# An output stage without transpositions: normalising attention in its own layout, with inverted sums spread by one bf16 product

## What is computed

```python
h = _layernorm(x) * (1 + ca) + sa
# attention with rope and causal mask, per head of 16 channels
scores = einsum('bhid,bhjd->bhij', q, k) / sqrt(16), masked
out = einsum('bhij,bhjd->bhid', softmax(scores), v) @ Wo + bo
x = x + ga * (h + out)                    # per batch: ga is a row of 256
h = _layernorm(x) * (1 + cb) + sb
x = x + gb * experts(h)                   # 8 experts, 512 tokens each
```

## Time and profile before

| | us |
|---|---|
| median of three runs | 3014.26 (3013.57 to 3014.30) |
| the profiled execution | 3013.66 |
| its span | 3011.9 |

### The profile page before, as it was taken

How to read it: one execution, slowest core, us unless ns; L and a number is a source line. 1 busy time by engine, 2 the same in 40 slices (tenths; PEclk the granted TensorE clock), 3 DMA queues, 4 the chain that set the end, 5 groups by cost and what they waited for, 6 DMA issues and landing times. The chain is left out here.

```text
span 3011.9 us, 48208 instructions
## 1 busy us (share of the span) xinstructions
PE 2753.8 (91%) x17467; PEld 1341.3 (45%) x17467; DVE 2140.9 (71%) x3145; ACT 1825.3 (61%) x3739; POOL 974.6 (32%) x1298
## 2 busy tenths in 40 slices
PE   1788889499999999999999999999999879998997
PEld 0454445234444444444444444444444346775664
DVE  4999999587777777777777777777777436652221
ACT  1676677157777777777777777777777744441121
POOL 1666666312212212212212212212211247771331
PEclk7899999689999999999999999999999989999999
DMA  3367676824454354454454455354345068962342
GB/s 97 119 221 231 220 233 210 214 50 93 87 108 93 88 106 94 87 106 94 88 105 95 89 104 99 86 103 98 88 102 102 25 227 291 312 224 58 99 109 44
DMA packets 186485, 384.09 MB, mean 128 GB/s; under 512 B 33397, under 2 KB 102421, under 8 KB 173736
## 3 DMA queue, kind: packets, MB, share of 16 engines
q1 hardware_dynamic: 180106, 372.48, 48.2%
q0 software_dynamic: 6144, 8.52, 1.6%
HBM read 238.55 MB, written 144.53 MB: 127 GB/s over the span
## 5 line engine op out<-in xcount | busy, mean ns | idle before, releaser
L929 DVE TENSOR_REDUCE mx<-ps 128x2 f32<-128x1024 f32 (+3 forms) x1216 | 1371.5, 1167 | 396.9 <-PE ps L1017 301.7
L975 ACT ACTIVATE prob<-ps 128x512 f32<-128x512 f32 (+1 forms) x2560 | 1251.8, 560 | 538.8 <-PE ps L1035 530.1
L1010 PE MATMUL ps<-k_rows,q_rows 96*128 96x512 bf16 (+3 forms) x3072 | 911.2, 332 | 41.0 <-DMA k_rows<-k_parts 34.4
L1035 PE MATMUL ps<-q_rows,k_rows 99*128 99x512 bf16 (+3 forms) x3072 | 907.2, 328 | 14.7 <-ACT prob L975 6.1
L868 POOL TENSOR_SCALAR_AFFINE_SELECT prob<-prob 128x512 f32<-128x512 f32 x512 | 320.0, 637 | 1451.3 <-ACT prob L975 1451.3
L1054 PE MATMUL ps<-prob,v_rows 128*32 128x512 f32 (+3 forms) x6144 | 628.3, 496 | 0.0
L1035 PEld LDWEIGHTS ps<-q_rows,k_rows 99*128 99x128 bf16 x3072 | 273.1, 98 | 599.0 <-ACT prob L975 360.3
L1010 PEld LDWEIGHTS ps<-k_rows,q_rows 96*128 96x128 bf16 x3072 | 290.2, 98 | 271.4 <-DVE mx L929 60.5
L1017 PE MATMUL ps<-mask_b,unit_b 128*128 128x128 bf16 (+2 forms) x1408 | 348.6, 248 | 0.0
L673 PE MATMUL ps<-x_t,w_all 128*128 128x512 f32 x512 | 249.8, 634 | 0.0
L1054 PEld LDWEIGHTS ps<-prob,v_rows 128*32 128x32 f32 x6144 | 134.3, 108 | 245.8 <-ACT prob L975 122.9
(11 more groups left out here) (154 smaller groups left out, 2678.1 us busy)
## 6 DMA issues: line engine op xcount, KB each, us to landing
k_rows<-k_parts SPq DMA_DIRECT2D x384, 128.0 KB, 7.3
v_ones<-v_st SPq DMA_DIRECT2D x64, 512.0 KB, 4.3
v_rows<-v_ones SPq DMA_DIRECT2D x64, 512.0 KB, 9.1
att<-o_sb SPq DMA_DIRECT2D x128, 256.0 KB, 2.4
att_b<-att SPq DMA_DIRECT2D x16, 2048.0 KB, 10.1
q_parts<-stage SPq DMA_DIRECT2D x128, 192.0 KB, 3.3
k_parts<-stage SPq DMA_DIRECT2D x128, 192.0 KB, 3.3
q_rows<-q_parts SPq DMA_DIRECT2D x64, 384.0 KB, 4.6
```

Source lines behind the costliest of these rows:

```text
L929: dve.tensor_reduce(dst, src, AX.X, ALU.max).then_inc(a_free, 1)
L975: nc.scalar.activation(prob[:, (g * NPC + i) % RING, h, 0:w], src, ACT.Exp).then_inc(exp_done, 1)
L1010: ins = pe.matmul(ps[:, at, col:col + w], q[0:ROWS, g, h, i * P:(i + 1) * P], k[0:ROWS, g, h, k0:k0 + w], start=(r == 0), stop=True, skip_ ...
L1035: ins = pe.matmul(ps[:, PS_B + bank(g, n), at:at + w], k[0:AUG, g, h, j * P:(j + 1) * P], q[0:AUG, g, h, q0:q0 + w], start=True, stop=True)
```

## The change

The output stage keeps tokens along the columns throughout, as `att_d` has them and as the output product wants them, so nothing is transposed and the copy of L1332 goes. Attention rows and sums are loaded apart. The sums of a batch come as 128 partitions of 128 columns, are inverted there in one instruction, split in three bf16 parts, stored to DRAM and loaded again as 48 rows (3 parts x 16 heads) of 1024 tokens. A product of these 48 rows with a constant matrix of ones and zeros puts each head's inverse on the 16 rows of its channels in PSUM, 512 tokens at a time, two such products for the two halves of the channels, so four a batch. VectorE multiplies the attention rows with it. Inverses are formed three batches ahead, products of spread inverses and normalising run one batch ahead of the output product, in between its tiles.

The depth of the output product's PSUM ring grows from 2 banks to 4, x is kept for 3 batches and not 4, the residual may run two batches ahead of the sums, in place of ScalarE's two tiles ahead of its copies. The residual's instructions, the norm of the chosen tiles and the experts stay as they are.

```diff
@@ SP's queue @@
+            def load_den(b):
+                reuse(sp, inverted, b - 1)
+                sums = att_d[b].rearrange("g (h n) t -> (g h) n t", n=2 * DH)[:, DH, :]
+                sp.dma_start(den[:, b % 2, :], sums.rearrange("h (a c) -> h a c", c=P)).then_inc(den_in[b % 2], DMA)
+            def save_inv(b):
+                sp.wait_ge(inv_done, b + 1)
+                sp.dma_start(rec_d[b].rearrange("s h (a c) -> (h a) s c", c=P), inv3[:, b % 2]).then_inc(inv_stored[b % 2], DMA)
+            def load_rec(b):
+                sp.wait_ge(inv_stored[b % 2], (b // 2 + 1) * DMA)
+                reuse(sp, spread, (b - RR + 1) * NQ)
+                sp.dma_start(rec[:, b % RR, :], rec_d[b].rearrange("s h t -> (s h) t")).then_inc(rec_in[b % RR], DMA)
+            def load_num(b):
+                reuse(sp, norm_done, (b - 1) * NQ)
+                for k in range(KC):
+                    mine = att_d[b, k * NG // KC:(k + 1) * NG // KC].rearrange("g (h n) t -> (g h) n t", n=2 * DH)
+                    sp.dma_start(num[:, b % 2, k, :], mine[:, 0:DH, :]) \
+                      .then_inc(num_in[b % 2], DMA)
...
+            load_den(0)
+            load_den(1)
+            load_small(0)
+            load_num(0)
+            save_inv(0)
+            load_den(2)
+            load_rec(0)
+            load_x(0)
+            save_inv(1)
+            load_num(1)
...
             for b in range(B):
+                if b + 2 < B:
+                    load_small(b + 2)
+                    load_num(b + 2)
+                if b + 3 < B:
+                    save_inv(b + 3)
+                if b + 4 < B:
+                    load_den(b + 4)
                 if b + XR - 1 < B and b >= 1:
-                    load_x(sp, b + XR - 1)
+                    load_x(b + XR - 1)
+                if b + 3 < B:
+                    load_rec(b + 3)
...
+                store(b)
@@ VectorE @@
+            def invert(b):
+                p = b % 2
+                dve.wait_ge(den_in[p], (b // 2 + 1) * DMA)
...
+                dve.reciprocal(inv[:, p, :], den[:, p, :]).then_inc(inverted, 1)
...
+                dve.tensor_copy(inv3[:, p, 0, :], inv[:, p, :]).then_inc(inv_hi, 1)
...
+                dve.tensor_tensor(inv_rest[:, p, :], inv[:, p, :], inv3[:, p, 0, :], ALU.subtract).then_inc(inv_left, 1)
...
+                dve.tensor_copy(inv3[:, p, 1, :], inv_rest[:, p, :]).then_inc(inv_mid, 1)
...
+                dve.tensor_tensor(inv3[:, p, 2, :], inv_rest[:, p, :], inv3[:, p, 1, :], ALU.subtract).then_inc(inv_done, 1)
+            def normalise(b, q):
...
+                dve.wait_ge(spread, b * NQ + q + 1)
+                dve.tensor_tensor(n_t[:, b % 2, k, at], num[:, b % 2, k, at], ps[:, PS_R + q % 2, :], ALU.mult) \
+                   .then_inc(norm_done, 1)
...
+            for b in range(B):
+                if b + 1 < B:
+                    scale_weights(b + 1)
+                for t in range(T):
+                    if t == 1 and b + 3 < B:
+                        invert(b + 3)
+                    finish(b, t)
+                    prepare((b - SB) * T + t)
+                    if t % 2 == 1 and b + 1 < B:
+                        normalise(b + 1, t // 2)
@@ ScalarE @@
-                    reuse(act, x2_done, b * T - T)
+                reuse(act, x2_done, (b - 2) * T + t + 1)
...
-                    nc.scalar.copy(n_t[:, t % 2], ps[:, PS_T + t % 2, 0:D].rearrange("p (k n) -> p k n", k=KC)) \
-                      .then_inc(nt_copied, 1)
@@ TensorE @@
+            def spread_rec(b, q):
...
+                pe.matmul(ps[:, PS_R + q % 2, :], mine, rec[:, b % RR, half * HALF:(half + 1) * HALF],
+                          start=True, stop=True).then_inc(spread, 1)
+            def product(b, t):
...
+                pe.matmul(o, ones3[:, :], ob[:, b % 4, :], start=True, stop=False)
+                for k in range(KC):
+                    ins = pe.matmul(o, n_t[:, b % 2, k, t * P:(t + 1) * P], wg[:, b % 2, k, :], start=False,
+                                    stop=(k == KC - 1))
...
+            for b in range(B):
+                for t in range(T):
+                    product(b, t)
+                    if t % 2 == 0 and b + 1 < B:
+                        spread_rec(b + 1, t // 2)
```

More of the change, by code:

```diff
@@ L1147, in phase3 @@
         pair = lambda n: (sem(n + "0"), sem(n + "1"))
[L1148 to L1158, removed]
+        num = sb("num", [P, 2, KC, L], F32)
+        den = sb("den", [P, 2, P], F32)
+        inv = sb("inv", [P, 2, P], F32)
+        inv_rest = sb("inv_rest", [P, 2, P], F32)
+        inv3 = sb("inv3", [P, 2, 3, P], BF16)
+        rec = sb("rec", [3 * HEADS, RR, L], BF16)
+        rows = sb("head_rows", [3 * HEADS, HEADS, DH], BF16)
+        unit3 = sb("unit3", [3 * HEADS, HEADS], F32)
         st = sb("st4", [P, NT, 6], F32)
@@ L1177, in phase3 @@
         block = ctx.enter_context(nc.Block())
[L1179 to L1184, removed]
-        def load(sp, b, p):
-            sp.dma_start(gate[:, p], mods_d[b, M_GA, :].partition_broadcast(P)).then_inc(small_in[p], DMA)
-            sp.dma_start(ob[:, p], out_bias_d[b]).then_inc(small_in[p], DMA)
-            sp.dma_start(att[:, p], att_d[b].rearrange("g p t -> p g t")).then_inc(att_in[p], DMA)
@@ L1200, in store @@
+            def store(b):
                 sp.wait_ge(x2_done, b * T + T)
-                sp.dma_start(dst.rearrange("(t p) d -> p t d", p=P), x2[:, p]).then_inc(stored[p], DMA)
+                dst = sum_d[b * L:(b + 1) * L] if b < SB else out[b]
+                rows2 = ffn.x2[:, b * T:(b + 1) * T, :] if b < SB else x2[:, b % 2]
+                sp.dma_start(dst.rearrange("(t p) d -> p t d", p=P), rows2).then_inc(stored[b % 2], DMA)
             def load_chosen():
@@ L1298, in _ @@
-            loop(dve, work)
+            for b in range(2):
+                invert(b)
+            dve.wait_ge(unit_in, 3 * DMA)
+            dve.tensor_copy(rows[:, :, :], unit3[:, :].rearrange("p (h o) -> p h o", o=1)
+                            .to_broadcast([3 * HEADS, HEADS, DH])).then_inc(rows_done, 1)
+            invert(2)
+            scale_weights(0)
+            for q in range(NQ):
+                normalise(0, q)
+            for b in range(B):
[8 more added lines that the diff above has]
+                        normalise(b + 1, t // 2)
@@ L1401, in _ @@
-            loop(pe, work)
+            def spread_rec(b, q):
+                k, half = q % KC, q // KC
+                n = b * NQ + q
+                if q == 0:
+                    pe.wait_ge(rec_in[b % RR], (b // RR + 1) * DMA)
+                reuse(pe, norm_done, n - 1)
+                mine = rows[:, k * (HEADS // KC):(k + 1) * (HEADS // KC), :].rearrange("p h n -> p (h n)")
+                pe.matmul(ps[:, PS_R + q % 2, :], mine, rec[:, b % RR, half * HALF:(half + 1) * HALF],
+                          start=True, stop=True).then_inc(spread, 1)
```

170 lines of the change are left out of this document (79 added, 91 removed).

## The result

The changed kernel takes 3038.37 us (median of four runs, 3035.77 to 3041.27) against 3014.28 for the kernel before on the same chip: ratio 1.0078, 95% interval 1.0066 to 1.0091. It is 24 us slower where 34 us faster was forecast. The profiled execution took 3038.47 us (span 3036.4).

A forecast was written before the change was run, and what follows sets the result against it. GpSimd was to become the output stage's bound in TensorE's place: start 2445.4 + work 218.7 + collisions 10.4 + lag 5 + last sum 0.5 + what follows 300.6 = 2980.6, said as 2980 us, range 2964 to 3000.

The forecast's parts named there:

- The step that failed: Output stage, DMA: a batch moves 3.66 MB, at 333 GB/s 11.0 us, hidden with 2 us to spare.
- The second step that failed: SP's queue: waits after the start are covered, since x is issued two batches, some 25 us, before GpSimd wants it.
- rival (b): Output stage: DMA or SP's order bounds; 2990 us at 265 GB/s, 3000 with waits on top; chance 0.13.
- its work with the collisions: GpSimd in the output stage: 218.7 us of work, plus 10.4 us for collisions with thirteen inverts.
- its waits: GpSimd in batches 2 and 3: a lag behind VectorE's bn_stats and bn_aggr comes due, 5 us, from 0 to 8.
- what follows: Everything after the output stage's last sum: 300.6 us, not touched by the change.
- TensorE: Output stage: 1.27 us a tile without transpositions, four spreading products 1.3 us a batch; sum 11.4 us a batch.
- Rival (c): TensorE, now waiting for others in each tile, is granted the lower clock; 3036 us; chance 0.05.
- Rival (d): Inverses aren't there when TensorE spreads them, each batch waits some 3 us; about 3010 us, no change; chance 0.04.
- VectorE: Output stage: reciprocal 0.95 us, normalising pieces 0.687 us each, invert with collisions 3 us a batch.
- Collision with GpSimd: Beside VectorE's invert GpSimd loses 0.43 of the other's length, 0.8 us an invert, 10.4 us in all, from 4 to 31.
- Start: Output stage: GpSimd starts at 2445.4, 2 us later than before, as x waits behind the first inverses; bounds 2444 and 2448.

The follow-up runs named there:

- e8: Changed kernel with channels ordered (n, head), so the outermost dimension of each attention load is 16 and not 8; 2983.9 us.
- e4: Changed kernel with five idle products of 48 rows and 256 columns behind each tile; 3231.6 us.
- e5: Changed kernel with five idle products of 128 rows and 256 columns behind each tile, on values of the output weights; 3049.8 us.
- e13: Changed kernel with only the bias product padded by zeros from 3 rows to 128; 3040.9 us.
- e14: e8 with two idle products of 128 rows and 256 columns behind each tile; 2985.6 us.
- e2: Changed kernel with a batch's attention rows in sixteen loads of 16 rows in place of two; 3004.4 us.

## Why the prediction was wrong

**The step that failed** is the DMA's: "3.66 MB, at 333 GB/s 11.0 us ... Hidden, with 2 us to spare". The rate was read from loads of another shape. The new attention loads have 8 heads as the outermost dimension of their source, and while they run almost alone the share is 0.51 and the rate 173 GB/s, against 1.01 and 405 for the old ones. In the stage the 3.66 MB went at 227 GB/s, which makes 16.1 us a batch and not 11.0. The Trainium skill (DMA: Bandwidth & Descriptors, "Why a DMA increments its semaphore by 16 and not by 1") says that a transfer is dealt to as many engines as the largest number up to 16 that divides the slowest dimension of both its sides, here 8. This case's trace agrees: the share is 0.51, and the single change of that dimension to 16 brought it to 1.03 and gave 54.6 us. Both loads of a batch are on the way in that stretch and the share is still a half, which speaks for the same eight engines. What the loads take from the eight engines that all transfers need can be estimated: of 3.66 MB a batch 1.05 lie on one half alone, so that half carries 1.05 + 2.61 / 2 = 2.35 MB, as if 4.7 MB were moved, more than the 4.45 of before. The saving in bytes, on which the DMA sum rested, was gone. And 333 GB/s was too high even for loads on all engines: e8 has 273 in the stage, 13.4 us a batch. In the packets of the trace a row of 4 KB took 161 ns in the mean while the old loads ran alone (2434 to 2437 us), 183 after (2436 to 2441), 269 in e8 (2435.5 to 2440).

**The second step that failed**: "Later waits of this kind are covered: SP issues x two batches, some 25 us, before GpSimd wants it". The residual now runs up to two batches ahead of the sums itself, so this lead is spent: from SP's issue of x to the moment when GpSimd is through with the batch before, the trace has 12.1 us (median of batches 3 to 15; 42.9 in the kernel before). ScalarE could start only 15.7 us after the issue, and GpSimd waited 66.5 us in 12 batches, 5.5 each. In e8 the two are 13.2 and 10.2, and the wait is nearly gone. SP's wait for the store of the inverses in each round, 83.7 us in all, stood in rival (b) and was put at nothing in the sum: the prediction had the 9.0 us landing of small stores and used it only for the start.

By the sum's own terms, as times of the last sum:

| term | forecast | after | e8 |
|---|---|---|---|
| GpSimd's start | 2445.4 | 2450.05 | 2449.39 |
| its work with the collisions | 229.1 | 217.9 | 218.4 |
| its waits | 5 | 66.5 | 14.6 |
| to the end of the last sum | 0.5 | 2.5 | 0.5 |
| last sum ends | 2680.0 | 2737.0 | 2682.9 |
| what follows | 300.6 | 301.5 | 300.6 |

- **TensorE**: 1.27 us a tile at the high level is right (the sums of the last tiles of the kernel after stand 1.27 apart). A tile with a spreading product takes 1.59, so such a product costs 0.32, the 0.22 and 0.1 of the sum. The clock was not priced: with the transpositions it stood at 1.00, without them at 0.78. That their 128 rows had kept it up is argued from e4 and e5; no run shows it.
- **Rival (c)**, chance 0.05, named the fall of the clock and drew the wrong consequence. The clock did fall, to 0.78 of full speed. Waiting, the reason that (c) gave, isn't enough: in e4 TensorE hardly waited (busy 222 of 230 us) and the level was low throughout. And a stage that waits for DMA hides it: with 37 us less to do for TensorE (e13) the time moved by +2.1. That the measured 3038 lies near (c)'s 3036 is chance. The argument against (c), the clock of 0.91 at 31 of 40 us busy, did not carry over: TensorE was busy for the same 78% here, with other products.
- **Rival (b)**, chance 0.13, named the right place, DMA and SP's wait for the store, and priced it at 2990 to 3000, from the average rate of the old transfers. Its own rate was again one of full spread. The measured 227 GB/s was below every rate that it took.
- **Rival (d)**, chance 0.04: its sum is wrong in itself. Sixteen batches at 3 us are 48 us and not the 30 that it adds.
- **VectorE**: the reciprocal took 950 ns (0.95 forecast), the normalising 674 (0.687). The five steps of an invert came to 2.63 us in the mean, in e8 to 3.02 (3 forecast).
- **Collision with GpSimd**: over-sized. The row at 2559.35, from which 0.43 was taken, has the addition itself stretched from 0.415 to 0.76 us (it starts at 2558.92), and at its median of 0.748 it was mostly VectorE that lost. From before to after the mean of the residual's operations went from 753 and 731 ns to 753 and 735, that of the scalings from 728 to 794: 1.6 us in all, where 10.4 were put in. In e8 it is 2.3.
- **Start**: 2449.4 to 2450.05 for 2445.4. The store of the first inverses, issued at 2435.12, landed after 7.3 us and not 3.1, behind the loads of `num`, and x after it.

```profile
2435.12 0.38 SPq L1198 DMA_DIRECT2D rec_sums<-inv  x1
...
2442.44 0.30 SPq L1203 DMA_DIRECT2D rec<-rec_sums  x1
...
2450.05 0.73 POOL L1413 TENSOR_TENSOR res_b<-res_b,a_b 128x256 f32<-128x256 f32 x1 [20.32 <-ACT res_b L1384]
```

The forecast of 2980 was thus the time of another kernel: with loads on all engines (e8) 2983.9 was measured, with GpSimd as the bound as the prediction had it. Luck has a part in this nearness: the start is 4 us late and the waits 9.6 us longer, while the collision is some 10 us smaller. In e8 the DMA share is 0.97 beside GpSimd's 203 of 230 us, at 273 GB/s and not 333; so there is no spare DMA time left, and which of the two holds the stage was not told apart. Left open too: why a row of the attention loads takes longer in e8, so that its rate stays under 333 GB/s, and whether a mended order of SP's queue could win back the 4 us of the start without making the inverses late.

## What to carry to other kernels

A DMA rate from the trace holds only for transfers of the same shape: before a sum rests on it, compare the outermost dimension of the new source with the old one, and read a stretch in which one kind of transfer runs alone; a share near a half is the sign. Where a load's lead is the cover, count it from its issue to the moment when its reader is ready, with the landings of the new queue. A lowered clock, like a long wait, is a cause only if the time moves when it alone is lifted; here 37 us less on TensorE (e13), and a clock of 0.92 for 0.83 (e14), took nothing off the kernel. And an edit that is meant to lift the clock may shorten the work as well: compare the pace of a tile at the same granted clock first.

## What the runs showed of the hardware that I had not expected

- TensorE busy for 97% of the time, with idle products of 48 rows beside main products of 128, was granted the low level for the whole stretch (e4, 0.50); with idle products of 128 rows and other values it was granted 0.93 (e5).
- A bf16 product of 3 rows costs the products beside it more than one of 128 rows. Padded with zeros, it is as long itself (311 ns in the mean, 312 before), but a tile goes from 1.27 to 0.97 us at a granted clock of 1.00 and from 2.33 to 1.90 at 0.50 (kernel after and e13).
- SP was held by the issue of the 128 KB scale row for 4.6 us in the median in the kernel before, 4.9 in the kernel after, 1.1 in e8 and 0.58 in e2. The same issue can cost its engine eight times as much; that it depends on what is queued ahead is a guess.
- With casts and subtractions on VectorE beside it, GpSimd lost 0.1 to 0.2 us per invert in the mean, against 0.8 worked out from a single row; the loss fell on VectorE instead, where a subtraction of 293 ns alone took 482 in the mean.
